# Layer 1 of a graph network: three groups of 128 edges in a turn read their source rows from SBUF in place of two, VectorE doing one of them, and the turned one-hot becomes a compare with a scalar per partition

## The reference

```
e_in     = concat(x[src], x[dst])                       # per edge, 256 numbers
edge_new = relu(e_in @ We1 + be1) @ We2 + be2           # per edge, 128 numbers
agg      = segment_sum(edge_new, dst)                   # per node
mesh     = relu(concat(x, agg) @ Wn1 + bn1) @ Wn2 + bn2
out      = layernorm(x + (x + mesh))
```

## Time and profile before

| | |
|---|---|
| median of 3 runs | 4099.13 us |
| the profiled execution | 4090.99 us, span 4088.8 us |
| layer 0 | 0 to about 2080 us |
| nodes' tables for layer 1 | about 2080 to 2179 us |
| layer 1, first to last gather | 2179.3 to 4059.7 us, 1507 gathers |
| behind the last gather | 29 us |
| busy in the whole span | TensorE 71%, VectorE 61%, ScalarE 61%, GpSimd 73% |

### The profile page before, as it was taken

How to read it: one execution, slowest core, us unless ns; L and a number is a source line. 1 busy time by engine, 2 the same in 40 slices (tenths; PEclk the granted TensorE clock), 3 DMA queues, 4 the chain that set the end, 5 groups by cost and what they waited for, 6 DMA issues and landing times. The chain is left out here.

```text
span 4088.8 us, 90253 instructions
## 1 busy us (share of the span) xinstructions
PE 2902.8 (71%) x18890; PEld 2648.6 (65%) x18891; DVE 2493.5 (61%) x5568; ACT 2497.4 (61%) x10068; POOL 2964.7 (73%) x3137
## 2 busy tenths in 40 slices
PE   6888888888888788888865565655556565666656
PEld 4877777777777777777744555555556555555656
DVE  4877777777777777777765444444444555555544
ACT  3767777777777677777646555455555555555553
POOL 5777777777777777777536777777777777777775
PEclk8999999999999999999987777767767777777777
DMA  6333333333333333333234333333333333333332
GB/s 190 81 81 81 83 81 81 81 82 81 82 80 82 81 84 81 81 81 83 57 108 108 95 90 94 94 91 94 90 94 94 93 99 94 98 97 95 97 99 63
DMA packets 426429, 367.97 MB, mean 90 GB/s; under 512 B 276875, under 2 KB 355163, under 8 KB 426108
## 3 DMA queue, kind: packets, MB, share of 16 engines
q0 software_dynamic: 98240, 214.20, 20.4%
q1 hardware_dynamic: 316720, 143.31, 14.0%
q10 hardware_dynamic: 11214, 8.17, 0.7%
HBM read 343.89 MB, written 21.44 MB: 89 GB/s over the span
## 5 line engine op out<-in xcount | busy, mean ns | idle before, releaser
L724 POOL DMA_INDIRECT he<-h_table,src_i x1563 | 1480.7, 947 | 514.9 <-issue 504.3
L1744 POOL DMA_INDIRECT msg<-p_table,src x1507 | 1422.3, 944 | 467.1 <-issue 461.6
L1777 PE MATMUL p_sumT<-msg,hot 128*80 128x129 f32 x3136 | 595.7, 369 | 688.2 <-ACT sumT L1830 683.7
L1777 PEld LDWEIGHTS p_sumT<-msg,hot 128*80 128x80 f32 x3136 | 542.5, 215 | 725.4 <-issue 533.9
L1622 ACT COPY picked<-hT 128x1 f32 x7168 | 759.9, 187 | 412.4 <-issue 398.3
L1762 PE MATMUL p_edge<-r_win,hotT 80*128 80x128 f32 x3136 | 480.0, 312 | 59.7 <-DVE msg L1899 45.8
L763 PE MATMUL p_score<-qk_two,heT 128*128 128x160 f32 x1568 | 396.7, 336 | 165.4 <-ACT heT L873 163.4
L1762 PEld LDWEIGHTS p_edge<-r_win,hotT 80*128 80x128 f32 x3136 | 452.6, 227 | 63.7 <-issue 63.2
L1899 DVE TENSOR_TENSOR msg<-msg,p_edge 128x512 f32<-128x512 f32 x392 | 243.6, 662 | 377.5 <-DMA msg<-p_table,src 376.4
L765 PE MATMUL p_score<-qk_win,heT 128*128 128x80 f32 x3136 | 465.2, 273 | 0.0
L765 PEld LDWEIGHTS p_score<-qk_win,heT 128*128 128x128 f32 x3136 | 454.3, 200 | 0.0
(11 more groups left out here) (210 smaller groups left out, 4565.5 us busy)
## 6 DMA issues: line engine op xcount, KB each, us to landing
dst_row<-in_dst_dram SPq DMA_DIRECT2D x196, 320.0 KB
feat<-in_edge_attr_dram SPq DMA_DIRECT2D x196, 128.0 KB
he<-h_table,src_i POOLq DMA_INDIRECT x1563
msg<-p_table,src POOLq DMA_INDIRECT x1507
qk_win<-qk_table SPq DMA_DIRECT2D x196, 40.0 KB
qk_two<-qk_table SPq DMA_DIRECT2D x392, 20.0 KB
r_win<-r_table SPq DMA_DIRECT2D x196, 40.0 KB
qk_table<-qk SPq DMA_DIRECT2D x13, 512.0 KB
```

The lines of the kernel that those rows point to most:

```text
L724: e.indirect_dma_start(out=he[u][:, j, 2 * FE:2 * FE + ROW], out_offset=None, in_=h_table[:, :], in_offset=bass.IndirectOffsetOnAxis(ap=sr ...
L1744: e.indirect_dma_start(out=msg[u][:, j, 0:D], out_offset=None, in_=p_table[:, :], in_offset=bass.IndirectOffsetOnAxis(ap=src_i[u][:, j:j + ...
L1777: mm = e.matmul(p_sumT[:, :], hot_of(c)[:, j, :], msg[u][:, j, 0:D + 1], start=(j == 0), stop=(j == J - 1))
```

## The change

Slots 5, 0 and 3 have a picked group now. ScalarE makes slots 5 and 3, VectorE slot 0. In turn 0 only slot 5 is picked. Up to 24 numbers are read into registers at once, and the picks of VectorE stand between its `hots` and its `boths`, in the first five steps of a turn. The partition's number is added to the chunks' starts once a round (`node_b`), and the turned one-hot is one compare of `dst_row` with a column of it.

```diff
-PICKED = (5, 1)
-BATCH = 8
-BY_ACT = P // BATCH
+PICKED = (5, 0, 3)
+BY_ACT = (P, 0, P)
+BY_DVE = tuple(P - n for n in BY_ACT)
+AT_ONCE = 24
...
+            node_c = sb("node_c", [W, 1], ctx=ctx)
+            node_b = sb("node_b", [W, NCH], ctx=ctx)
...
-                        return PICKED.index(c[1]) if at_first and c[1] in PICKED else None
+                        g = PICKED.index(c[1]) if at_first and c[1] in PICKED else None
+                        return None if g and isinstance(c[0], int) and c[0] == 0 else g
...
-                        for b in range(first, first + n):
-                            at = b * BATCH
+                        start = first + (0 if of is BY_ACT else BY_ACT[g])
+                        parts = -(-n // AT_ONCE)
+                        ends = [start + n * k // parts for k in range(parts + 1)]
+                        for at, to in zip(ends, ends[1:]):
                             _, nodes = nc.values_load_multi_w_load_instructions(
-                                picks_i[g][0:1, at:at + BATCH], engines=(engine,), min_val=0, max_val=N - 1,
+                                picks_i[g][0:1, at:to], engines=(engine,), min_val=0, max_val=N - 1,
...
-                            for k in range(BATCH):
+                            for k in range(to - at):
                                 op = copy(picked[g][:, at + k:at + k + 1], x1T[:, bass.ds(nodes[k], 1)])
...
-                        per = -(-len(PICKED) * of // SLOTS)
+                        per = -(-sum(of) // (SLOTS if of is BY_ACT else SLOTS - 2))
...
-                            if u == 2 and not (isinstance(i, int) and i == 0):
+                            if u == 0 and not (isinstance(i, int) and i == 0):
+                                load_picks(2, i)
+                            elif u == 3 and not (isinstance(i, int) and i == 0):
                                 load_picks(0, i)
-                            elif u == 5 and not (isinstance(i, int) and i == TURNS - 1):
+                            elif u == 4 and not (isinstance(i, int) and i == TURNS - 1):
                                 load_picks(1, i + 1)
...
-                            pick_first(e, mybir.EngineType.Activation, e.copy, picked_act, BY_ACT)
...
-                            e.scalar_tensor_tensor(out=hotT_of(c)[:, j0:J, :], in0=dst_row[u][:, j0 * P:CH].rearrange(row_j, j=J - j0),
-                                                   scalar=start_b[0:W, bass.ds(number(c), 1)], in1=p_node.unsqueeze(2).broadcast_to([W, J - j0, P]),
-                                                   op0=ALU.subtract, op1=ALU.is_equal).then_inc(hotT_done, 1)
+                            e.tensor_scalar(hotT_of(c)[:, j0:J, :], dst_row[u][:, j0 * P:CH].rearrange(row_j, j=J - j0),
+                                            node_b[:, bass.ds(number(c), 1)], None, ALU.is_equal).then_inc(hotT_done, 1)
...
                         def step(c):
                             if not is_last(c):
                                 hots(shift(c, 1))
+                            if at_first:
+                                pick_step(e, mybir.EngineType.DVE, e.tensor_copy, picked_dve, c, BY_DVE)
                             boths(c)
...
+                        e.tensor_scalar(node_b[:, :], start_b[0:W, :], node_c[:, 0:1], None, ALU.add).then_inc(fixed, 1)
```

More of the change, by code:

```diff
@@ L1464, in gnn_kernel @@
             p_sum = ctx.enter_context(nc.psum_tensor("p_sum1", [P, 2, W], F32))
-            p_nodes = ctx.enter_context(nc.psum_tensor("p_iota", [P, W + 1], F32))
-            p_iota, p_node = p_nodes[:, 0:W], p_nodes[0:W, W:W + 1]
+            p_iota = ctx.enter_context(nc.psum_tensor("p_iota", [P, W], F32))[:, :]
             p_hid = ctx.enter_context(nc.psum_tensor("p_hid", [P, 512], F32))
@@ L1475, in gnn_kernel, with made @@
             picked_act = sem("picked_act")
-            def pick_number(g, turn):
-                return turn * len(PICKED) + (g - 1) % len(PICKED)
+            picked_dve = sem("picked_dve")
+            def made(of, g, turn):
+                each = sum(n > 0 for n in of)
+                upto = sum(n > 0 for n in of[0:g + 1])
+                return turn * each + (upto + each if g == 0 else upto)
             in_win_done = sem("in_win_done")
@@ L1629, in pick_step @@
[L1629 to L1632, removed]
-                            turn = c[0] if g == 0 else c[0] + 1
-                            if not (isinstance(turn, int) and turn == TURNS):
-                                pick_columns(e, engine, copy, done, g, turn, at - g * of, n, of)
-                            at += n
@@ L1638, in pick_first @@
-                    def pick_first(e, engine, copy, done, of):
-                        pick_columns(e, engine, copy, done, 1, 0, 0, of, of)
+                        per = -(-sum(of) // (SLOTS if of is BY_ACT else SLOTS - 2))
+                        at, end = c[1] * per, min((c[1] + 1) * per, sum(of))
+                        for g in range(len(of)):
+                            low = sum(of[0:g])
+                            first, n = max(at - low, 0), min(end - low, of[g]) - max(at - low, 0)
+                            turn = c[0] if g == 0 else c[0] + 1
+                            if n > 0 and not (isinstance(turn, int) and turn == TURNS):
+                                pick_columns(e, engine, copy, done, g, turn, first, n, of)
@@ L1659, in load_picks @@
                             if not isinstance(turn, int) or turn > 0:
-                                before = val(e, pick_number(g, turn) - len(PICKED) + 1)
-                                e.wait_ge(picked_act, before)
-                                e.sem_inc(passed, 1)
+                                for done, of in ((picked_act, BY_ACT), (picked_dve, BY_DVE)):
+                                    if of[g]:
+                                        e.wait_ge(done, val(e, made(of, g, turn - 1)))
+                                        e.sem_inc(passed, 1)
                             at = val(e, (turn * SLOTS + PICKED[g]) * CH)
@@ L1713, in _ @@
                         if at_first:
-                            for g in (1, 0):
-                                load_picks(g, 0)
+                            load_picks(0, 0)
                         for u in range(1, SLOTS):
@@ L1763, in edges @@
                                     if j == 0 and g is not None:
-                                        ready = val(e, pick_number(g, c[0]) + 1)
-                                        e.wait_ge(picked_act, ready)
+                                        for done, of in ((picked_act, BY_ACT), (picked_dve, BY_DVE)):
+                                            if of[g]:
+                                                e.wait_ge(done, val(e, made(of, g, c[0])))
                                         mm = e.matmul(p_edge[0][:, 0, :], picked[g][:, :], we1[:, 0, :], start=False, stop=True)
@@ L1846, in _ @@
                         if at_first:
+                            e.sem_inc(picked_act, sum(n > 0 for n in BY_ACT))
                             e.sem_inc(hid_done, 1)
-                            pick_first(e, mybir.EngineType.Activation, e.copy, picked_act, BY_ACT)
                             chunks(e, step, grouped=step_grouped)
@@ L1882, in hots @@
                             if j0:
[L1883 to L1887 removed]
+                                e.tensor_scalar(hotT_of(c)[:, 0, :], dst_row[u][:, 0:P], node_b[:, bass.ds(number(c), 1)], None, ALU.is_equal)
+                            e.tensor_scalar(hotT_of(c)[:, j0:J, :], dst_row[u][:, j0 * P:CH].rearrange(row_j, j=J - j0),
+                                            node_b[:, bass.ds(number(c), 1)], None, ALU.is_equal).then_inc(hotT_done, 1)
                         def boths(c):
@@ L1921, in _ @@
                             e.wait_ge(fixed, 2)
-                            e.tensor_reduce(p_node, node_sq[:, :], AX_X, ALU.add).then_inc(fixed, 1)
+                            e.tensor_reduce(node_c[:, :], node_sq[:, :], AX_X, ALU.add).then_inc(fixed, 1)
                             e.wait_ge(fixed, 3)
@@ L1933, in step_grouped @@
                                 normal(e, k)
+                        e.tensor_scalar(node_b[:, :], start_b[0:W, :], node_c[:, 0:1], None, ALU.add).then_inc(fixed, 1)
+                        e.wait_ge(fixed, val(e, FIXED + 1 + r))
                         hots((0, 0))
                         if at_first:
+                            e.sem_inc(picked_dve, sum(n > 0 for n in BY_DVE))
                             e.sem_inc(y_done, 1)
```

15 lines of the change are left out of this document (9 added, 6 removed).

## The result

The change makes the kernel slower by almost a fifth: **4826.95 us** (median of 4 runs, 4821.63 to 4827.65) against 4099.75 (4093.38 to 4100.48), ratio 1.1775 [1.1755, 1.1795]. The direction of the prediction holds; its size does not: +57.5 us forecast, +727 measured, far outside the range.

A forecast was written before the change was run, and what follows sets the result against it. GpSimd's gathers were taken to bound layer 1; -32.5 us for gathers removed and +90 for the one-hot's port holds gave +57.5, 4157 us for the median. The forecast's own range was 4138 to 4198, for all rivals 4062 to 4196.

The forecast's parts named there:

- What bounds the kernel: Layer 1: GpSimd's gathers follow each other at 1.2486 us each and set the time; the other engines have room.
- Gathers removed: Layer 1 on GpSimd: 26 gathers fewer, 1481, at 1.2486 us each, -32.5 us if GpSimd keeps its pitch.
- The register loads: Loads of src numbers for the picks: 13 numbers about 0.8 us, ten on VectorE 8.1 us a turn; cost nothing.
- The added waits and the order: VectorE's slot 0 and ScalarE's slot 3: sums and relu come some 7 us late, hidden by 57 us of buffers.
- VectorE's picks: 128 copies a turn on VectorE at 0.10 us each, 12.8 us, off the path and costing nothing.
- The one-hot: New compare on VectorE and the gathers stop each other: 0.92 us holds cost 0.46 us each, 196 times, +90 us.
- the early need: A gather needs the port about 0.13 us after its start and waits for VectorE's instruction to end.
- the late hold: A gather holds something VectorE's instructions need for its last 0.25 us, from 0.69 to 0.94 after its start.
- Rival 3: VectorE becomes the bound through copies, loads and stalls, 71 us a turn: +100 us, 4199; chance 0.06.
- Rivals 1 and 2: New one-hot takes no port: 4067, chance 0.22; or holds it only briefly, 0.54 us: about 4104, chance 0.20.

The follow-up runs named there:

- e10: Changed kernel with aligned loads, the old one-hot, VectorE's picks behind boths, copy_sums ahead of ScalarE's picks, relu_hidden and roots behind the step: 4056.87 us, ratio 0.9908.
- e12: The whole changed kernel, its register loads and one-hot kept, with only the order on the engines made that of e10: 4324.80 us, ratio 1.0554.
- e1: Changed kernel with every register load starting at a multiple of four and taking a multiple of four numbers: 4187.26 us, ratio 1.0213.
- e11: e10 with the change's new one-hot in place of the old one: 4122.99 us, ratio 1.0062.
- e6: e3 with the 8 rows of the one-hot made as two compares, of 1 and 7 rows: 4100.56 us, ratio 1.0005.
- e3: The kernel before with the change's new one-hot alone: 4174.36 us, ratio 1.0181.

## Why the prediction was wrong

1. **What bounds the kernel**: right. GpSimd's pitch was the bound, and e10 shows it again.
2. **Gathers removed**, -32.5: right where GpSimd keeps its pitch, -32.2 in e10. The change itself broke the condition.
3. **The register loads: the step that failed.** The prediction put a further number at 38 to 42 ns, 13 numbers at 0.8 us, VectorE's loads at 8.1 us a turn (for ten; they are nine), and ScalarE's at less than before for being fewer. That slope came from two rows, one number and eight, and the eight start at a multiple of four in all 896 loads that the trace had of them. The new starts do not. Measured: 2.95 us for 13 numbers, 21.6 us a turn on VectorE; 44.8 in place of 17.5 on ScalarE. This is a price of kind and not of size, and the rows of before could not show it; the diff could, since the starts (18, 37, 13, 26) stand in it, and a bound from both sides should have reached up to each number at the price of a load of one, 0.28 to 0.30 us. The Trainium skill (Runtime: NRT & Kernel Launch, "Instruction fetch mechanics") gives about 200 ns a register even for bulk register loads, from HBM; the loads off a multiple of four agree (0.215 to 0.226, from SBUF), those on it are three times cheaper, which that page does not have. An estimate from that page's figure is 0.2 x 384 = 77 us of loads a turn on both engines, above the 66.4 that are measured.
4. **The added waits and the order**, cost 0, "hidden by 57 us": failed too. The 57 us of buffers cover a delay that comes once; a loop that takes longer than the gathers' pitch in every turn uses them up (in e12, it seems, after seven turns) and then sets the time. The prediction counted VectorE's and ScalarE's time apart, 55.6 us here and "hardly changes" there, and compared each with the turn. But `copy_sums` stood behind ScalarE's picks, the adds behind VectorE's, and each engine waits for the other once a chunk, so their picks and loads add. With good loads the change's order costs 64 us (e1 against e11); with the change's loads 502 (e12). The loads cost 202 in the good order and 640 in the change's. Each of the two makes the other dear; together they are 704 of the 727. The other 23 are nearly the sum of the gathers saved and the one-hot's price, the +26 of e11.
5. **VectorE's picks**: 13 copies mostly take 1.53 us, their starts 0.114 apart; over all of them it is 0.104, for 0.10 assumed, and ScalarE's 0.093 as before. The term is right.
6. **The one-hot**: the mechanism is right in both halves, the early need and the late hold, and so is the time of the compare of 8 rows (1.15 us). 0.46 us was forecast for each, 0.52 to 0.59 measured. Wrong was that compares of 7 rows would run two at once: they do not, and hold nothing. 114 compares pay and not 196: +59 in place of +90.
7. **The rivals.** Rival 3 had the right place, VectorE (with ScalarE) in front of the sums, and the right sign in the row that would show it (GpSimd waiting for the sums), but was priced by copies and stalls at +100 and given 0.06. Rivals 1 and 2 fall: the port is taken, for 1.15 us.

In short, for a kernel with aligned loads and the picks behind the work that others wait for, the sum would have had the right terms and the right sign, but twice the size: +57.5 against e11's +26, mostly because the 82 compares of 7 rows hold nothing. That the change is slower, as forecast, is luck in part: 704 of its 727 us come from two terms that the prediction put at nothing.

## What to carry to other kernels

Before an instruction's price is stretched from a trace to another size, look whether its start and its length keep the form they had there: here the same eight numbers cost 0.55 or 1.75 us by one place of their start. Work that "has room" on two engines is only free if it stands behind what the other engine waits for; add the times along the loop from engine to engine, not for each engine by itself. And a buffer hides a delay once, not one that comes every turn.

## What the runs showed of the hardware

- A register load from SBUF that starts at a multiple of 16 bytes takes 0.55 us for 8 numbers and 1.26 for 20 on ScalarE, 1.62 for 24 on VectorE; one that does not takes about 0.22 us for each number (8: 1.75 and 18: 3.87 on ScalarE, 13: 2.95 on VectorE).
- A one-source compare on VectorE with 8 rows of 128 runs at 1.15 us and lengthens the gathers by some 0.55 us each time; with 7 rows it runs at 1.81 us and lengthens none. So a slower instruction made the kernel faster (e6 against e3). That the evenness of the row count decides was not tried with other counts.
